# Perceiver layer on one core: the bias of the similarities as a VectorE product over rows instead of TensorE products over columns

## The reference, cut to what matters

```python
hc = layernorm(x)                         # "normed" in the kernel
w1, w2, w3 = w_sim[:d], w_sim[d:2 * d], w_sim[2 * d:]
Sim = (hc @ w1)[:, :, None] + (hq @ w2)[:, None, :] + einsum('bid,bjd->bij', hc * w3, hq) + b_sim[0]
A = softmax(Sim, axis=2)
hq_hat = einsum('bij,bjd->bid', A, hq)
Batt = softmax(max(Sim, axis=2), axis=1)
hc_bar = einsum('bi,bid->bd', Batt, hc)
feats = concatenate([hc, hq_hat, hc * hq_hat, hc * hc_bar], axis=-1)
x = x + feats @ W_qv + b_qv
```

## Time and profile before

| | us |
|---|---|
| median of 3 runs (lowest, highest) | 112.34 (112.3, 112.38) |
| the profiled execution, its own time | 112.1 |
| its span, first to last instruction | 110.3 |
| TensorE busy (matmuls) | 105.1 |
| VectorE busy | 93.1 |
| ScalarE busy | 82.4 |
| GpSimd busy | 29.3 |
| granted TensorE clock, mean | 1.000 |

### The profile page before, as it was taken

How to read it: one execution, slowest core, us unless ns; L and a number is a source line. 1 busy time by engine, 2 the same in 40 slices (tenths; PEclk the granted TensorE clock), 3 DMA queues, 4 the chain that set the end, 5 groups by cost and what they waited for, 6 DMA issues and landing times.

```text
span 110.3 us, 1855 instructions
## 1 busy us (share of the span) xinstructions
PE 105.1 (95%) x582; PEld 86.4 (78%) x583; DVE 93.1 (84%) x152; ACT 82.4 (75%) x171; POOL 29.3 (27%) x47
## 2 busy tenths in 40 slices
PE   5999999999999999999999999999999998998890
PEld 2368768588858888899899999989898997887680
DVE  1478999999998998999999999999999847674352
ACT  5067668899979989999999899988976725903450
POOL 2239200444043314233242424286330000200100
PEclk9999999999999999999999999999999999999999
DMA  2999999999999999999999999960000000000001
GB/s 72 367 406 423 416 422 422 416 422 422 409 420 417 418 415 423 417 420 442 442 389 423 415 422 425 406 260 0 3 0 0 0 6 0 0 0 0 6 3 48
DMA packets 8220, 29.82 MB, mean 270 GB/s; under 512 B 1042, under 2 KB 1298, under 8 KB 8082
## 3 DMA queue, kind: packets, MB, share of 16 engines
q1 hardware_dynamic: 8064, 29.69, 66.3%
q10 hardware_dynamic: 146, 0.01, 0.1%
HBM read 29.57 MB, written 0.13 MB: 269 GB/s over the span
## 4 chain that ended last, share of the span: by engine, by line
PE 94%; DVE 1%; issue 1%; ACT 1%; DVEq 0%; ACTq 0%
PE mixed_ps L997 18%; PE scores_ps L968 10%; PE mixed_ps L999 9%; PE scores_ps L940 8%; PE scores_ps L944 8%; PE scores_ps L954 8%; PE scores_ps L925 7%; PE scores_ps L910 4%; PE scores_ps L979 3%; PE scores_ps L1090 2%; PE mixed_ps L1142 2%; PE side_ps L1016 1%; PE scores_ps L1155 1%; PE side_ps L1133 1%; PE scores_ps L1016 1%; PE scores_ps L1125 1%
## 5 line engine op out<-in xcount | busy, mean ns | idle before, releaser
L698 DVE TENSOR_TENSOR pair<-raw,pair 128x1024 fp32r<-128x1024 f32 (+2 forms) x42 | 49.0, 1183 | 1.3 <-ACT pair L488 1.0
L488 ACT ACTIVATE pair<-raw 128x512 fp32r<-128x512 f32 (+1 forms) x42 | 34.5, 820 | 3.8 <-DMA raw<-keys_dram 3.4
L997 PE MATMUL mixed_ps<-pair,turned_high 128*128 128x512 f32 x84 | 32.3, 418 | 0.0
L999 PE MATMUL mixed_ps<-pair,turned_low 128*128 128x256 f32 x84 | 23.6, 281 | 0.0
L463 POOL CAST pair<-raw 128x512 fp32r<-128x512 f32 x22 | 13.6, 619 | 27.3 <-DVE pair L698 23.1
L997 PEld LDWEIGHTS mixed_ps<-pair,turned_high 128*128 128x128 f32 x84 | 15.8, 188 | 2.8
L520 ACT ACTIVATE turned_high<-scores_ps 128x512 fp32r<-128x512 f32 (+1 forms) x23 | 13.4, 584 | 4.0 <-PE scores_ps L968 4.0
L721 DVE TENSOR_SCALAR_CACHE_REDUCE neg_scores<-scores_ps,neg_max 128x1024 f32<-128x1024 f32 (+1 forms) x13 | 15.8, 1216 | 0.2
L999 PEld LDWEIGHTS mixed_ps<-pair,turned_low 128*128 128x128 f32 x84 | 16.0, 190 | 0.0
L728 DVE TENSOR_TENSOR turned_low<-scores_ps,turned_high 128x512 fp32r<-128x512 f32 (+1 forms) x23 | 15.3, 667 | 0.2 <-ACT turned_high L520 0.2
L968 PE MATMUL scores_ps<-ident,neg_scores 128*128 128x128 f32 x98 | 14.6, 272 | 0.0
(11 more groups left out here) (189 smaller groups left out, 130.6 us busy)
## 6 DMA issues: line engine op xcount, KB each, us to landing
raw<-keys_dram SPq DMA_DIRECT2D x24, 512.0 KB, 10.0
raw<-rows_dram SPq DMA_DIRECT2D x24, 512.0 KB, 9.2
w<-weights_dram SPq DMA_DIRECT2D x1, 1792.0 KB, 9.9
w<-weights_dram SPq DMA_DIRECT2D x2, 512.0 KB, 10.4
const<-const_dram SPq DMA_DIRECT2D x1, 832.0 KB, 11.5
raw<-keys_last_dram SPq DMA_DIRECT2D x1, 256.0 KB, 10.2
raw<-rows_last_dram SPq DMA_DIRECT2D x1, 256.0 KB, 6.8
x_sb<-x_dram SPq DMA_DIRECT2D x1, 128.0 KB, 2.2
```

The source lines that it names most:

```text
L488: nc.scalar.activation(pair[:, use % PAIR_BUFS, 0, 0:columns], raw[:, slot(item), 0:columns], ACT.Copy)\
L698: nc.vector.tensor_tensor(out=pair[:, use % PAIR_BUFS, 1, 0:columns], in0=raw[:, slot(item), 0:columns], in1=pair[:, use % PAIR_BUFS, 0, 0 ...
L997: nc.tensor.matmul(mixed_ps[:, :].rearrange("p (h d) -> p h d", h=2), probs_high, both[:, :, t * D:(t + 1) * D], start=(k == EARLY and t = ...
L999: last = nc.tensor.matmul(mixed_ps[:, 0:D], probs_low, rows_tile(high, t), start=False, stop=(k == LATE - 1 and end))
```

## The change

The weights w1 and the number b_sim are repeated in all 128 rows of the constants, in columns 1664 to 1920, and a row of the constants in HBM becomes 2048 numbers (8 KB). SyncE loads these 257 columns (1028 bytes in each of 128 partitions) in a transfer of their own right behind key chunk 14. VectorE multiplies `normed` with them and sums over the row, between low 18 and low 19. The three TensorE products, the tensor `bias` and its transfer go. `sim_max` becomes an instruction with three operands in SBUF. TensorE's wait for sim_max_done stands now right ahead of the product that reads `sim_max`.

```diff
-C_MASK, C_COS, C_SIN, C_BK, C_BV, C_COS_T, C_SIN_T, C_ALL = 0, *(P + D * n for n in range(7))
+C_MASK, C_COS, C_SIN, C_BK, C_BV, C_COS_T, C_SIN_T, C_W1 = 0, *(P + D * n for n in range(7))
+C_ROW = 2048
...
-        const = sb("const", [P, C_ALL])
+        const = sb("const", [P, C_W1])
...
-        bias = sb("bias", [1, 1])
+        w1_rows = sb("w1_rows", [P, D + 1])
+        hw1_parts = sb("hw1_parts", [P, D])
+        hw1_sum = sb("hw1_sum", [P, 1])
...
-        hw1_ps = mixed_ps[:, 0:1]
...
                     sp.dma_start(w[:, 4 * part:4 * part + 4, :], blocks_in[:, 4 * part:4 * part + 4, :])\
                         .then_inc(w_qv_loaded[part], 16)
+                if k == 14:
+                    sp.dma_start(w1_rows[:, :], const_in[:, C_W1:C_W1 + D + 1]).then_inc(w1_rows_loaded, 16)
...
-                    sp.dma_start(const[:, :], const_in).then_inc(const_loaded, 16)
+                    sp.dma_start(const[:, :], const_in[:, 0:C_W1]).then_inc(const_loaded, 16)
...
-            act.dma_start(bias[:, :], bias_in).then_inc(bias_loaded, 16)
...
             for e, chunks in enumerate(evictions):
                 for k in chunks:
+                    if k + 2 == 19:
+                        dve.wait_ge(w1_rows_loaded, 16)
+                        dve.wait_ge(normed_done, DH)
+                        nc.vector.scalar_tensor_tensor(hw1_parts[:, :], normed[:, :], 1.0, w1_rows[:, 0:D], ALU.mult,
+                                                       ALU.mult, accum_out=hw1_sum[:, :]).then_inc(hw1_done, 1)
                     if k + 2 < CHUNKS and not is_native(k + 2):
                         keys_low(k + 2)
                 running_max(e)
...
-            nc.vector.tensor_tensor(out=sim_max[:, :], in0=hw1_ps, in1=neg_max[:, EVICTIONS:EVICTIONS + 1],
-                                    op=ALU.subtract).then_inc(sim_max_done, 1)
+            nc.vector.scalar_tensor_tensor(sim_max[:, :], hw1_sum[:, :], w1_rows[:, D:D + 1],
+                                           neg_max[:, EVICTIONS:EVICTIONS + 1], ALU.add, ALU.subtract)\
+                .then_inc(sim_max_done, 1)
...
                 scores(k)
-                if k == 1:
-                    pe.wait_ge(ones_set, 1)
-                    pe.wait_ge(vec_loaded, 16)
-                    pe.wait_ge(bias_loaded, 16)
-                    pe.wait_ge(normed_t_done, DH)
-                    for a in range(DH):
-                        nc.tensor.matmul(hw1_ps, normed_t[:, a, :], vec[:, VC_W1 + a:VC_W1 + a + 1],
-                                         start=(a == 0), stop=False)
-                    nc.tensor.matmul(hw1_ps, ones[0:1, :], bias[0:1, 0:1],
-                                     start=False, stop=True).then_inc(hw1_done, 1)
...
-            pe.wait_ge(sim_max_done, 1)
             for k in range(EARLY, CHUNKS):
                 if k + 2 < CHUNKS:
                     turn(k + 2)
                 if k == EARLY + 1:
-
+                    pe.wait_ge(sim_max_done, 1)
                     nc.tensor.matmul(batt_ps[:, 0:P], sim_max[:, 0:1].to_broadcast([P, P]), ident[:, :],
                                      start=True, stop=True).then_inc(sim_max_spread, 1)
...
-def constants(bk, bv):
+def constants(bk, bv, w1, b_sim):
-    c = np.zeros((P, C_ALL), np.float32)
+    c = np.zeros((P, C_ROW), np.float32)
+    c[:, C_W1:C_W1 + D], c[:, C_W1 + D] = w1, b_sim
```

More of the change, by code:

```diff
@@ L57, with build @@
 VC = VC_B + 2 * DH
-C_MASK, C_COS, C_SIN, C_BK, C_BV, C_COS_T, C_SIN_T, C_ALL = 0, *(P + D * n for n in range(7))
-def build(nc, x, keys_in, keys_last_in, rows_in, rows_last_in, weights_in, vec_in, bias_in, const_in, out):
+C_MASK, C_COS, C_SIN, C_BK, C_BV, C_COS_T, C_SIN_T, C_W1 = 0, *(P + D * n for n in range(7))
+C_ROW = 2048
+def build(nc, x, keys_in, keys_last_in, rows_in, rows_last_in, weights_in, vec_in, const_in, out):
     keys_full = keys_in.rearrange("(k p) n -> k p n", p=P)
@@ L237, in build @@
         vec_loaded = sem("vec_loaded")
-        bias_loaded = sem("bias_loaded")
+        w1_rows_loaded = sem("w1_rows_loaded")
         w_qv_loaded = [sem(f"w_qv_loaded{n}") for n in range(2)]
@@ L1216 @@
         "vec": np.concatenate(columns, axis=0).T,
-        "bias": a["L0_xattn_b_sim"].reshape(1, 1),
-        "const": constants(a["L0_attn_bk"], a["L0_attn_bv"]),
+        "const": constants(a["L0_attn_bk"], a["L0_attn_bv"], a["L0_xattn_w_sim"][0:D], a["L0_xattn_b_sim"]),
     }
```

## The result

| | us |
|---|---|
| median of 6 runs (lowest, highest) | 113.61 (112.83, 113.87) |
| the kernel before, median of 6 runs beside it | 112.32 |
| ratio to before, 95% interval | 1.0115 [1.0086, 1.0145] |
| the profiled execution, its own time | 113.44 |
| its span (before: 110.3) | 111.6 |

The kernel is slower by 1.15%, 1.3 us. The forecast was 112.74 with a range up to 113.0: the direction was right, the size was not, and the median lies outside the range. The profiled span grew by 1.3 us as well. A few runs of this program are disturbed (ratios leave them out, medians do not), and of the profiled executions of f1, g3, h2 and h4, which have a mean clock of 0.985, only the transfers are read.

What follows compares the result with a forecast made beforehand. It took the chunk 19 landing, through high 19 and VectorE, to bound TensorE at low 22. TensorE 0, transfer +0.4 and VectorE 0 gave 112.34 + 0.4 = 112.74 us, range 112.25 to 113.0.

Steps and rivals of the forecast that it cites:

- What bounds the kernel: Near 40 us TensorE meets VectorE at low 22; VectorE is set by high 19, that by chunk 19's landing.
- the 0.4 to 1 that was forecast: Sign of being right: TensorE holes between 10 and 40 us sum to 0.4 to 1 us, mostly waiting for VectorE.
- TensorE's products, 0: Removing L1045 and L1047 near 10 us frees 0.65 us of TensorE, worth 0 at the end.
- The rival in which 0.65 us comes through: The wait at low 22 is no real limit, so TensorE's saving is gained: 111.7 us; 6 in 100.
- VectorE's product, 0.45 in a hole of 0.47: The new product and sum, about 0.45 us, fits VectorE's hole ahead of low 19, widened by 0.4: cost 0.
- the 0.06 of the forecast: Ahead of the row chunks' low parts, `sim_max` grows from 0.158 us by at most 0.06, costing 0.
- The new transfer, +0.4: Behind key chunk 14, 131.6 KB delays chunk 19 and all behind by 0.4 us (bounds 0.31 and 1.25), passed to the end.
- The rival in which it costs more: Transfer costs 0.8 to 1.25 us, from its row pitch or nearly full-priced packets: 113.1 to 113.6; 9 in 100.
- the 0.052 us of a packet of x: Price per packet from x's rows of about 1 KB; eight packets per engine give the new transfer 0.41 us.
- The prediction's other estimate from that page: By the skill's transfer sizes the new transfer would take 1.3 us, the kernel near 113.6; rejected for a full queue.
- The rest, together: TensorE's moved wait, the `bias` transfer and `const` from rows with a new pitch: 0 in all.
- The absorbed transfer: An instruction fetch near 28.4 us falls elsewhere, so chunk 19 lands as before: 112.25 to 112.45 us; 20 in 100.

Runs made afterwards that it cites:

- f1: The changed kernel again, no edit, on another chip: 113.91 us, 1.0113 of the kernel before.
- g3: The kernel before plus the new transfer issued three times, read by nothing, rows 8 KB apart, old tile addresses: 116.71 us, 1.0381.
- h2: The kernel before plus the new transfer alone, read by nothing, constants with rows of 8448 bytes, old tile addresses: 112.9 us, 1.0044.
- h4: The changed kernel with `raw` at 51200, a multiple of 256, and constants with rows of 8448 bytes: 112.62 us, 1.0022 of the kernel before.
- f3: The kernel before with `raw` moved by 32 bytes to 48928 and the tiles behind it by 64: 113.37 us, 1.0088.
- f4: The changed kernel without the new transfer, tile addresses as before, VectorE multiplying with x instead of w1: 112.23 us, 0.9995 of the kernel before.
- h3: The kernel before plus the new transfer alone, read from a tensor of its own with rows 1028 bytes apart: 112.69 us, 1.0046.
- e1: The kernel before with an unused tile ahead of x_sb, moving `raw` to 50976 and all tiles behind: 113.09 us, 1.0073.
- i2: The changed kernel with constants in rows of 8448 bytes, `raw` staying at 50976: 113.38 us, 1.0091 of the kernel before.
- i3: The changed kernel once more, no edit: 113.86 us, 1.0108 of the kernel before.
- g2: The kernel before plus the new transfer alone, read by nothing, rows 8 KB apart, old tile addresses; a repeat on another chip: 114.16 us, 1.0157.
- h1: The kernel before plus the new transfer alone, read by nothing, rows 8 KB apart, old tile addresses; another repeat: 113.14 us, 1.0065.
- e5: The kernel before with `const` read from rows of 8 KB, nothing else changed: 112.32 us, 1.0014.
- g1: The changed kernel with `raw` at 51072, 128 past a multiple of 256: 113.53 us, 1.0106 of the kernel before.
- f2: The changed kernel with `raw` at 51008, 64 past a multiple of 256: 113.62 us, 1.0109 of the kernel before.
- e3: The kernel before plus the new transfer alone, read by nothing, rows 8 KB apart, its tile behind all others: 113.28 us, 1.0047.

## Why the prediction was wrong, step by step

**What bounds the kernel: right for the trace after, and not the only road.** Landing of chunk 19, high 19, low 19, the low parts of 22 and 23, TensorE's load for low 22, the early mix: each moved by 1.27 to 1.34. TensorE's products stopped first at low 20, not low 22; between 9 and 42 us they stood 0.43 in sum, at the low end of the 0.4 to 1 that was forecast. A late queue can also reach the early mix through row chunk 2 and ScalarE, as f3 shows; the prediction had only the road through chunk 19.

**TensorE's products, 0: right.** f4 has them removed and neither the transfer nor the address: 0.9995. The rival in which 0.65 us comes through is refuted. A 94% share of the chain was no promise.

**VectorE's product, 0.45 in a hole of 0.47: right.** Its instruction took 0.41 and its read 0.08, overlapping, and low 19 in f4 starts as its read does. In the kernel after, 0.33 us stand idle behind it. (The prediction's example of neighbours that overlap shows none, 32.33 + 0.75 + 0.47 being 33.55 exactly; its rows at 38.92 and 40.73 do overlap, by 0.07, and the 0.45 stands.) It ran 1.1 us later than forecast, near 34.1, since low 18 itself came late and took 1.55 instead of 0.75. `sim_max` became 0.220 from 0.158, the 0.06 of the forecast, and cost nothing.

**The new transfer, +0.4: right in the trace after (0.37), not for this read in general.** With rows that do not lie 8 KB apart it takes 0.33; with rows that do, it took up to 1.6 in other traces. The rival in which it costs more "because its rows lie 8 KB apart" held a part of the truth and had 9 in 100, because I let the 0.052 us of a packet of x stand for a read that no row showed. The page "DMA: Bandwidth & Descriptors" of the Trainium skill, section "Latency and other measured facts", reports copies between HBM tensors slowed by row pitches of large powers of two: 103 GB/s at 4 MiB against 214 with 4 KiB of padding. The smallest pitch it lists is 512 KiB, with 207. The runs here show slow packets at a pitch of 8 KB, and none with 256 bytes more. What in the memory is behind it, no run shows. The prediction's other estimate from that page, 1.3 us by the sizes in the section "Bandwidth" of the Trainium skill, does not hold in a full queue: 0.33 in h2 and h3. That table is for transfers issued from GpSimd, which the prediction did not say. The 113.6 that it gave with this estimate is the time measured, by luck: of its 1.3 us the transfer took 0.37.

**"The rest, together": the step that failed.** It put everything outside the listed parts at 0. It went through what the change does to instructions and transfers, and held that all other transfers cost what they had cost. It said nothing of the addresses of the tiles, though the diff puts three of them ahead of the ring. The 4096-byte packets then cost 0.004 us more on the mean, 0.03 for a chunk. Between chunk 3 and the landing of chunk 19 there are 16 chunks and two parts of W_qv, 18 x 0.031 = 0.56 us. In runs the address alone is worth 0.8 to 1.0 us (0.73% in e1, 0.88% in f3, with intervals down to 0.4 and 0.6 us). Counted up to row chunk 2, where the second road leaves the queue, it has lost as much: from chunk 3 to there it took 32.59 us before, 33.38 in e1 and 33.62 in f3. By the two traces: 1.27 = 0.24 (first chunks) + 0.39 (pace, to chunk 14) + 0.37 (transfer) + 0.27 (pace and the fetch, to chunk 19). The 0.24 and about 0.1 of the last term are scatter of these two executions; the change explains some 0.9 of the 1.27 by this road.

With both mended, h4 takes 112.62 where the forecast had 112.74, so without the two costs that it did not have, the sum would have come out; h4's ratio, 1.0022, can't be told from 1 either.

**The absorbed transfer** (a fetch of instructions falls elsewhere) had 20 in 100. Such fetches do move, but in runs of one and the same kernel too; see below. It was not seen to give anything back for good: in i2 and i3 it fell behind chunk 19, which landed at 32.60 and 32.75, and the spans are 111.4 and 111.7 all the same. A dear transfer is in part taken back, though: from chunk 15 to chunk 19, with a fetch on the way, g2 took 6.44 and h1 6.61, where the kernel before took 7.02 and e5 6.94.

**The range** reached to 113.0. It left out most of the dear transfer, and allowed for no second cost on top of the transfer's.

## What to carry to other kernels

When a diff allocates a tile, write down where every tile behind it lands, above all those that a full DMA queue writes: here a ring that starts off a multiple of 256 bytes cost 2.5% of the DMA rate, and in the changed kernel more time than the new transfer did. When a small read is cut out of a wide constant, look at the pitch of its rows, and measure it more than once, since its cost scatters. And the share of an engine in the chain says where the time is, not where it can be won: ask at which wait the others meet it.

## What was not expected of the hardware

- **The start of the ring costs.** With `raw` at a multiple of 256 the 4096-byte packets take 0.159 us; with it 32, 64 or 128 past one, 0.163 on the mean. Chunks of 512 KB land 1.248 apart or 1.28, all the same for 32, 64 and 128. The Trainium skill, "DMA: Bandwidth & Descriptors", section "How a descriptor splits into AXI transactions", says that a read which does not start on a 256-byte boundary begins with a transaction from the boundary below; for 4096 bytes that would be one transaction more, however far off the start is. The traces agree in that 32, 64 and 128 cost the same. They do not agree with a fixed price for each packet: in the traces with the ring off, 24 to 41% of the packets still took 0.159. The page speaks of what is read, and here it was the place written that moved. And one destination goes against it: by the addresses in g1's expectation the tile `w` starts 128 past a multiple of 256 in all kernels, and in the trace of before the packets of W_qv took 0.159 like nearly all others; after, with `w` in the same place, the packets that ran while its first part came in took 0.163 on the mean. So what is shown is a price of the ring's address for the whole queue; a rule for any destination is not shown, and the mechanism stays open.
- **Rows 8 KB apart:** some packets of 1028 bytes took 0.1 to 0.34 us instead of 0.047, 4 to 25 of them where chunks landed 1.25 apart. Where chunks landed 1.28 apart there were mostly none (0 or 1 in after, f1, f2 and i3, 7 in g1). Why, and what in the memory makes them slow, stays open.
- **Fetches of instructions wander.** A fetch of 16 KB takes about 1 us on one DMA engine and makes what is landing then late. From chunk 15 to chunk 19 it takes 6.20 to 6.41 us in the 11 traces without a fetch on the way. In the 9 others it took 6.94 to 7.88, but in g2 and h1, already late by a dear transfer, only 6.44 and 6.61. Between 28 and 38 us it began at 28.4 before, 28.7 after, 33.5 in h4, 35.5 in e3 and 37.4 in i2; in one kernel it began at 28.3 (g2), 29.6 (h1) and 35.5 (e3). In f4, where it came behind chunk 19, that chunk landed at 31.57, 0.86 earlier, and the span was 0.3 shorter.
- **VectorE beside GpSimd: who starts second waits.** Low 18 on VectorE (128x576, from 32.59) took 1.55 instead of 0.75 while GpSimd made its own 448 columns of the same chunk, which ran at that time because high 18 had come late:

```profile
32.37 1.16 POOL L458 TENSOR_TENSOR pair<-raw,pair 128x448 fp32r<-128x448 f32 x1 [5.01 <-ACT pair L491]
```

VectorE had started 0.22 behind it. In f2 the same happened (0.27 behind, 1.51 us). In f1, i3 and g3 VectorE started first, by 0.05 to 0.11: it took its 0.75, and GpSimd's part took 1.66 to 1.72 instead of 1.16. In the trace after it cost nothing: laid end to end at 0.75, the product would only have waited longer behind it for high 19.
